# Attention key scores taken from 32 of the 128 partitions: one line of a two-layer transformer kernel

## The chip, the cores and the metric

The kernel runs on one core of one Trainium2 chip. The metric is device time in microseconds (us) of one execution. Engines are named PE (TensorE matmul), PEld (TensorE weight load, which the profile lists apart from the matmuls), DVE (VectorE), ACT (ScalarE), POOL (GpSimd) and SP (SyncE, whose queue issues most of the DMAs here).

## The reference, cut to what matters

The input is x of shape (4, 512, 128): four batches of 512 tokens. Layer 0 is causal attention with 16 heads of width 8, then a mixture of 8 experts; layer 1 is a linear recurrence with gates and two feed-forward blocks. Only the first attention is touched:

```
Q, K, V = (heads(WQ), heads(WK), heads(WV))          # (4, 16, 512, 8) each
score = jnp.einsum('bhqd,bhkd->bhqk', Q, K) / jnp.sqrt(jnp.asarray(D_K, x.dtype))
score = score + mask                                  # causal
score = score - jnp.max(score, axis=-1, keepdims=True)
score = jnp.exp(score)
score = score / jnp.sum(score, axis=-1, keepdims=True)
out = jnp.einsum('bhqk,bhkd->bhqd', score, V)
```

## The kernel before

**Steps.** The heads are worked in groups of four. Four batches of 512 tokens times four groups make 16 steps, numbered w (or G) from 0 to 15; g = w mod 4 is the group within its batch and b the batch. A batch is four tiles of 128 tokens.

**The padded operands.** A head has 8 numbers, but takes 32 partitions: 8 rounded values, again 8 rounded values, 8 of a low part, and 8 that carry padding (zeros or ones, and minus the row's maximum). So the four heads of a step fill 128 partitions. `QS` holds the queries of a step in this form, 128 partitions by 512 tokens. `QM` is `QS` plus minus the row maximum in the padding rows. `KP[:, w % 3, j, i, :]` holds the keys of token tile j and head i: the 32 partitions of head i are filled, the other 96 are zero. All three have the type float32r.

**Row scores** (`row_scores`, L1615) multiply `QS` of one query tile, as the stationary operand, with `KP` of one key tile and all four heads, 512 columns; ten such units make a step, four of them followed by a matmul that adds the causal mask (L1618). They go through three PSUM banks (0 to 2), and DVE takes the maximum over each (L1052).

**Key scores** (`key_scores`, L1631) do the same product turned round: the stationary operand is `KP` of one key tile and one head, and the moving operand is `QM`, from the tile's first query to the end. A step has 12 units n. Units 0 to 3 are key tile 0 of heads 0 to 3 (512 columns), units 4 to 7 are key tile 1 (384 columns), units 8 to 11 are key tiles 2 and 3 (one matmul of 256 columns and one of 128, into one bank). They use banks 3 to 5 in turn; unit n waits until ACT has taken the exponential of unit n - 3 (L679). The exponentials are the weights `PT`.

**Values** (`values`, L1643) multiply `PT` with the values `V` of a head: 128 rows and 32 output columns, four heads side by side in the four 32-partition parts of bank 6. These are plain float32, for which the trace lists two records each.

**Other PE work of a step:** four transposes of the maxima (`turn_max`, L1657), four of the outputs (`turn_out`, L1665), and in batches 1 to 3 the output projection, the transposes, the logits and the ranks of the batch before (L1671 to L1705).

**The order** of PE's work is written out by hand, L1738 to L1797, in this sequence for a step w:

```
turn_max(w), key_scores(w-1, 10), row_scores(w+1, 2), key_scores(w-1, 11), values(w-1, 1),
row_scores(w+1, 3), key_scores(w, 0), [times_wo | turn_normed | ranks], row_scores(w+1, 4),
key_scores(w, 1), row_scores(w+1, 5), key_scores(w, 2), row_scores(w+1, 6), key_scores(w, 3),
values(w-1, 2), values(w-1, 3), row_scores(w+1, 7), key_scores(w, 4), row_scores(w+1, 8),
key_scores(w, 5), turn_out(w-1), row_scores(w+1, 9), [project], values(w, 0), key_scores(w, 6),
key_scores(w, 7), [turn_heads | logits], key_scores(w, 8), row_scores(w+2, 0), key_scores(w, 9),
row_scores(w+2, 1)
```

In square brackets stands what only some steps have: `turn_heads` where w is 4, 8 or 12, `logits` where w is 6, 10 or 14. Step 15 has no row scores and step 14 has none of w+2.

Of the kernel before, what the change touches and what calls it, by code (L numbers as in the profile page):

```python
# [13 lines left out]
P = 128  # L14
NB = 4
TB = 4
SEQ = TB * P
# [19 lines left out]
ROWB = 3  # L37
KEYB = 3
# [70 lines left out]
def build(nc, d):  # L109
    ctx = ExitStack()  # L110
    with ctx:
# [95 lines left out]
        with ExitStack() as attention:  # L207
            def early(name, shape, dt=F32):
                return attention.enter_context(nc.sbuf_tensor(name, shape, dt))
# [8 lines left out]
            QM = early("QM", [P, 2, SEQ], F32R)  # L218
            KP = early("KP", [P, 3, TB, 4, P], F32R)
# [130 lines left out]
        bank = [ps[:, i, :] for i in range(8)]  # L350
# [1217 lines left out]
        def _(pe):  # L1568
# [53 lines left out]
            def key_scores(w, n):  # L1622

                c, i = n // 4, n % 4
                if n == 0:
                    pe.wait_ge(tp_free, TURNS["max", w] + 1)
                if NKU * w + n >= KEYB:
                    pe.wait_ge(exp_done, NKU * w + n - KEYB + 1)
                for j in KC[c]:
                    at = OFF[j] - OFF[KC[c][0]]  # L1630
                    mm = pe.matmul(bank[ROWB + n % KEYB][:, at:at + SEQ - j * P], KP[:, w % 3, j, i, :],  # L1631
                                   QM[:, w % 2, j * P:SEQ], start=True, stop=True)
                mm.then_inc(ts_full, 1)
            def values(w, j):

# [102 lines left out]
            for w in range(NW):  # L1738
# [3 lines left out]
                if w:  # L1742
                    key_scores(w - 1, 10)
                if rows_next:
                    row_scores(w + 1, 2)
                if w:
                    key_scores(w - 1, 11)
                    values(w - 1, 1)
                if rows_next:
                    row_scores(w + 1, 3)  # L1750
                key_scores(w, 0)
                if b and g == 1:
                    times_wo(b - 1)
# [308 lines left out]
            for t in (0, 1):  # L2062
                mm = pe.transpose(bank[6][:, t * P:(t + 1) * P], xp[:, t, :], ident)
            mm.then_inc(t_half, 1)
            pe.wait_ge(xp_done, 1)
            for t in (2, 3):
                mm = pe.transpose(bank[4][:, (t - 2) * P:(t - 1) * P], xp[:, t, :], ident)
# [110 lines left out]
```

## Time and profile before

| | us |
|---|---|
| median of 3 executions (lowest, highest) | 658.8 (657.65, 662.22) |
| the profiled execution, its own time | 656.35 |
| its span, from the first to the last instruction | 654.6 |
| TensorE clock granted, mean over the span | 0.965 of full speed |

| stretch of the span | what runs |
|---|---|
| 0 to 28 us | loads, first projections, first row scores |
| 28 to 212 us | the 16 steps of attention |
| 212 to 232 us | end of attention for the last batch |
| 232 to 323 us | the eight experts |
| 323 to 654.6 us | layer 1 |

The profile is of one execution. Matmuls are pipelined and their ends are modelled, so how long PE takes per matmul is read from the distance between the starts of two matmuls in a row, not from the duration of one. A weight load that starts at the same moment as the matmul before it was taken ahead, beside that matmul's work; one that starts with its own matmul was not.

### The profile page before, as it was taken

The numbers are of one execution on the slowest core, as the hardware profiler recorded it, in microseconds if no ns is written. First come the engines' busy times: TensorE is split into PE (matmuls) and PEld (weight loads), VectorE is DVE, ScalarE is ACT, GpSimd is POOL, SyncE is SP. The second block draws the span as 40 slices with busy tenths as digits, with TensorE's granted clock in tenths as the row PEclk, the third lists the DMA queues.
The fourth block names the chain that finished last, engine by engine and source line by source line (L and its number), as shares of the span: only waits on it lengthen the run. The fifth ranks groups of instructions, "written<-read, shape, count | busy, mean of one in ns | idle before, by whom it ended". The sixth has DMA issues, their size and how long they took to land.

```text
span 654.6 us, 9264 instructions
## 1 busy us (share of the span) xinstructions
PE 583.0 (89%) x3347; PEld 433.0 (66%) x3347; DVE 402.2 (61%) x958; ACT 316.2 (48%) x543; POOL 172.9 (26%) x185
## 2 busy tenths in 40 slices
PE   8889989999998379999649698899999999998997
PEld 3556556556564258787536476688778878786866
DVE  6778788798884511432248986884669556762430
ACT  4756566556665204534216243752575255643351
POOL 6112122452543630000058623611300041001100
PEclk9999999999999579999969798999999999999999
DMA  4773242243110455834111100100000000000000
GB/s 130 223 247 110 77 130 65 82 145 97 55 44 2 137 167 167 263 90 118 41 32 32 30 4 2 34 0 1 1 17 2 1 0 18 1 0 1 18 1 17
DMA packets 44926, 42.51 MB, mean 65 GB/s; under 512 B 4176, under 2 KB 34384, under 8 KB 44880
## 3 DMA queue, kind: packets, MB, share of 16 engines
q1 hardware_dynamic: 42544, 37.44, 18.8%
q0 software_dynamic: 2048, 4.20, 2.2%
q8 instruction: 27, 0.44, 0.3%
q10 hardware_dynamic: 288, 0.28, 0.2%
q14 instruction: 19, 0.16, 0.1%
HBM read 25.12 MB, written 16.78 MB: 64 GB/s over the span
## 4 chain that ended last, share of the span: by engine, by line
PE 66%; DVE 10%; ACT 7%; issue 6%; DMA 5%; POOL 4%; SPq 2%; DVEq 0%; POOLq 0%; ACTq 0%
PE ps L1945 7%; PE ps L1615 6%; PE ps L1898 5%; PE ps L1631 5%; PE ps L1643 5%; PE ps L1967 5%; PE ps L1968 4%; PE ps L1889 4%; PE ps L2048 4%; PE ps L2044 4%; PE ps L2045 4%; PE ps L1971 4%; PE ps L1961 2%; DMA XS<-xs_dram 2%; PE ps L1618 2%
## 5 line engine op out<-in xcount | busy, mean ns | idle before, releaser
L679 ACT ACTIVATE PT<-ps 128x384 f32<-128x384 f32 (+1 forms) x192 | 93.5, 529 | 69.9 <-PE ps L1631 67.5
L1052 DVE TENSOR_REDUCE pm<-ps 128x4 f32<-128x512 f32 x160 | 102.3, 681 | 10.0 <-PE ps L1615 9.4
L1615 PE MATMUL ps<-KP,QS 128*128 128x512 f32 x160 | 71.7, 452 | 7.9 <-DVEq L1045 2.5
L546 POOL TENSOR_SCALAR_AFFINE_SELECT PT<-PT 128x512 f32<-128x512 f32 x64 | 39.9, 636 | 129.1 <-ACT PT L679 129.1
L1631 PE MATMUL ps<-QM,KP 128*128 128x512 f32 (+3 forms) x256 | 69.1, 331 | 1.5 <-DVE QM L1066 1.1
L1631 PEld LDWEIGHTS ps<-QM,KP 128*128 128x128 f32 x256 | 43.8, 189 | 22.8 <-issue 12.6
L796 ACT ACTIVATE HT<-ps,cols 128x640 f32<-128x640 f32 x32 | 25.4, 795 | 54.8 <-PE ps L1889 54.8
L1615 PEld LDWEIGHTS ps<-KP,QS 128*128 128x128 f32 x160 | 29.8, 188 | 27.5 <-DVE pm L1052 11.5
L1414 DVE TENSOR_TENSOR_SCAN zero<-decay,OG 128x512 f32<-128x512 f32 x32 | 44.8, 1400 | 1.1
L1643 PE MATMUL ps<-PT,V 128*32 128x128 f32 (+3 forms) x512 | 44.6, 442 | 0.0
L521 POOL TENSOR_TENSOR rstd<-veps,mhalf 128x4 f32<-128x4 f32 x11 | 12.7, 1157 | 110.7 <-DVE veps L963 110.5
L1898 PE MATMUL ps<-W,HT 128*128 128x128 f32 x320 | 37.8, 277 | 2.9 <-ACT HT L796 2.9
L1898 PEld LDWEIGHTS ps<-W,HT 128*128 128x128 f32 x320 | 36.3, 192 | 4.8 <-ACT HT L796 4.8
L853 ACT ACTIVATE hF<-ps,cols 128x512 f32<-128x512 f32 x16 | 11.0, 689 | 56.1 <-PE ps L2048 56.1
L1889 PE MATMUL ps<-XST,W 128*128 128x320 f32 x128 | 36.5, 438 | 1.1 <-DVE XST L1315 1.1
L1409 DVE SCALAR_TENSOR_TENSOR OG<-ps,cols,vs 128x512 f32<-128x512 f32 x32 | 23.9, 748 | 18.6 <-ACT vs L832 14.1
L836 ACT ACTIVATE gs<-ps,half_bg 128x512 f32<-128x512 f32 x32 | 22.0, 688 | 25.7 <-PE ps L1971 25.5
L611 POOL DMA_INDIRECT G<-ys_dram,posG x8 | 7.6, 950 | 93.0 <-DMA ys_dram<-zero 90.8
L832 ACT ACTIVATE vs<-ps,cols 128x512 f32<-128x512 f32 x32 | 22.0, 688 | 20.0 <-PE ps L1971 19.8
L582 POOL DMA_INDIRECT G<-ys_dram,posG x24 | 29.6, 1234 | 6.8 <-issue 6.8
L1889 PEld LDWEIGHTS ps<-XST,W 128*128 128x128 f32 x128 | 22.4, 190 | 12.1 <-ACT HT L796 4.5
L1945 PEld LDWEIGHTS ps<-lwo,oT 128*128 128x128 f32 x256 | 29.1, 192 | 0.2
(300 smaller groups left out, 1309.2 us busy)
## 6 DMA issues: line engine op xcount, KB each, us to landing
qk_dram<-HL SPq DMA_DIRECT2D x24, 256.0 KB, 3.5
W<-in_eW SPq DMA_DIRECT2D x16, 256.0 KB, 3.6
QS<-qk_dram SPq DMA_DIRECT2D x15, 256.0 KB
KP<-qk_dram SPq DMA_DIRECT2D x60, 64.0 KB, 2.4
xs_dram<-zero SPq DMA_DIRECT2D x4, 640.0 KB, 3.5
XS<-xs_dram SPq DMA_DIRECT2D x8, 320.0 KB, 5.0
ys_dram<-zero SPq DMA_DIRECT2D x8, 320.0 KB, 2.9
whole_h_w<-in_h_w SPq DMA_DIRECT2D x2, 1024.0 KB, 9.7
```

What stands on the lines that cost most here:

```text
L546: g.affine_select(out=diag, in_=diag, pattern=[[0, 4], [1, P]], compare_op=ALU.is_ge, fill=0.0, base=0, channel_multiplier=-1).then_inc(se ...
L582: g.indirect_dma_start(out=G[:, b % 2, i, :], out_offset=None, in_=ys_dram, in_offset=bass.IndirectOffsetOnAxis(ap=posG[:, c:c + 1], axis= ...
L679: act.activation(PT[:, i, a:z], bank[ROWB + n % KEYB][:, 0:z - a], ACT.Exp, scale=float(DK) ** -0.5).then_inc(exp_done, 1)
L1052: v.tensor_reduce(pm[:, t, k, :], bank[n % ROWB].rearrange("p (i n) -> p i n", n=P), AXX, ALU.max).then_inc(row_free[n % ROWB], 1)
L1414: v.tensor_tensor_scan(st, decay[:, f:f + 1].to_broadcast([P, SEQ]), kv, 0.0, ALU.mult, ALU.add).then_inc(st_done, 1)
L1615: mm = pe.matmul(to, QS[:, G % 2, t * P:(t + 1) * P], KP[:, G % 3, k, :, :].rearrange("p i n -> p (i n)"), start=True, stop=t != k)
L1631: mm = pe.matmul(bank[ROWB + n % KEYB][:, at:at + SEQ - j * P], KP[:, w % 3, j, i, :], QM[:, w % 2, j * P:SEQ], start=True, stop=True)
L1643: mm = pe.matmul(bank[6][32 * i:32 * i + 32, j * P:SEQ], V[:, j * H + g * 4 + i, :], PT[:, i, OFF[j]:OFF[j + 1]], start=(j == 0), stop=(j ...
L1889: mm = pe.matmul(ps[:, 2 * (f % 2) + a, 0:HALF], W1[:, s, f * P:(f + 1) * P], XST[:, s, a * HALF:(a + 1) * HALF], start=True, stop=True)
L1898: mm = pe.matmul(bank[4 + j // 4][:, (j % 4) * P:(j % 4 + 1) * P], HT[:, s, f, j * P:(j + 1) * P], W2[:, s, f, :], start=(f == 0), stop=(f ...
L1945: mm = pe.matmul(bank[5][:, t * P:(t + 1) * P], src[:, f, t * P:(t + 1) * P], w[:, f, :], start=(f == 0 and t == 0), stop=(f == n - 1), sk ...
L1967: pe.matmul(to, high[n][:, cs], halves_of[:, 0, :], start=True, stop=False)
```

## The change

The two operands of the key scores' matmul are cut to the 32 partitions of head i. What is left out are products with the zeros of `KP`. `KP`, `QM`, their filling, the row scores and the order of the work stay as they are.

```
                 for j in KC[c]:
                     at = OFF[j] - OFF[KC[c][0]]
-                    mm = pe.matmul(bank[ROWB + n % KEYB][:, at:at + SEQ - j * P], KP[:, w % 3, j, i, :],
-                                   QM[:, w % 2, j * P:SEQ], start=True, stop=True)
+                    mm = pe.matmul(bank[ROWB + n % KEYB][:, at:at + SEQ - j * P], KP[32 * i:32 * i + 32, w % 3, j, i, :],
+                                   QM[32 * i:32 * i + 32, w % 2, j * P:SEQ], start=True, stop=True)
                 mm.then_inc(ts_full, 1)
```

## Rows read from the trace of the kernel before

**Rows 1.** The page: busy time by engine, and engines in 40 slices.
```profile
PE 583.0 (89%) x3347; PEld 433.0 (66%) x3347; DVE 402.2 (61%) x958; ACT 316.2 (48%) x543; POOL 172.9 (26%) x185
PE   8889989999998379999649698899999999998997
PEclk9999999999999579999969798999999999999999
```

**Rows 2.** Busy time in stretches; the first five each run between two groups of maxima transposes.
```profile
core 0: us, PE busy (x) PEld busy (x) DVE busy (x) ACT busy (x) POOL busy (x), PEclk, DMA share, GB/s
40.61:50.61 10.00, 10.00 (x72) 6.39 (x71) 8.68 (x17) 6.22 (x14) 2.27 (x4) 1.00 0.81 263
50.61:60.61 10.00, 10.00 (x72) 6.38 (x71) 8.20 (x17) 6.35 (x14) 2.49 (x5) 1.00 0.35 120
70.61:83.97 13.36, 12.38 (x80) 7.40 (x78) 8.87 (x18) 8.19 (x18) 2.72 (x5) 1.00 0.15 44
83.97:96.36 12.39, 11.50 (x80) 7.24 (x80) 10.69 (x29) 6.60 (x14) 3.27 (x5) 1.00 0.54 167
118.21:132.32 14.11, 12.94 (x79) 7.38 (x78) 10.26 (x25) 8.18 (x18) 7.54 (x10) 1.00 0.33 98
...
30.00:212.00 182.00, 173.37 (x1213) 108.25 (x1212) 144.72 (x376) 108.91 (x223) 58.83 (x84) 1.00 0.32 99
```

**Rows 3.** Instructions in order of time, step 1: same array shape.
```profile
start us, us, engine line op out<-in xcount [idle before <-releaser]
42.90 0.40 PE L1631 MATMUL ps<-QM,KP 128*128 128x512 f32 x1
42.90 0.19 PEld L1615 LDWEIGHTS ps<-KP,QS 128*128 128x128 f32 x1
43.14 0.39 PE L1615 MATMUL ps<-KP,QS 128*128 128x512 f32 x1
...
44.75 0.39 PE L1631 MATMUL ps<-QM,KP 128*128 128x512 f32 x1
```

**Rows 4.** The same view, into and out of the 32-column matmuls.
```profile
45.06 0.16 PEld L1643 LDWEIGHTS ps<-PT,V 128*32 128x32 f32 x8 [0.35 <-issue]
45.06 0.42 PE L1643 MATMUL ps<-PT,V 128*32 128x256 f32 x4
...
45.85 0.19 PEld L1615 LDWEIGHTS ps<-KP,QS 128*128 128x128 f32 x1 [0.20 <-issue]
45.85 0.50 PE L1615 MATMUL ps<-KP,QS 128*128 128x512 f32 x1
45.96 0.19 PEld L1631 LDWEIGHTS ps<-QM,KP 128*128 128x128 f32 x1
46.19 0.34 PE L1631 MATMUL ps<-QM,KP 128*128 128x384 f32 x1
```

**Rows 5.** The same view: a full group of values, then key scores.
```profile
47.79 1.06 PE L1643 MATMUL ps<-PT,V 128*32 128x512 f32 x8
...
48.24 0.61 PE L1643 MATMUL ps<-PT,V 128*32 128x512 f32 x4
48.78 0.79 PE L1631 MATMUL ps<-QM,KP 128*128 128x384 f32 x4
```

**Rows 6.** The same view: after a matmul of 128 columns, and full-array transposes.
```profile
50.03 0.19 PEld L1615 LDWEIGHTS ps<-KP,QS 128*128 128x128 f32 x1
50.09 0.44 PE L1615 MATMUL ps<-KP,QS 128*128 128x512 f32 x1
50.38 0.39 PE L1618 MATMUL ps<-mask,identr 128*128 128x512 f32 x1
...
50.61 0.27 PE L1657 MATMUL ps<-const,MX 128*128 128x128 f32 x1
```

**Rows 7.** Waits from 30 to 212 us: us in total, times, longest.
```profile
PEld ps L1615 <- DVE pm L1052: 10.6, 18, 1.3
PEld ps L1631 <- ACT PT L679: 3.8, 12, 0.8
PE ps L1615 <- DMA KP<-qk_dram: 1.9, 1, 1.9
```

**Rows 8.** The line of the key scores, its matmuls: count, and when.
```profile
L1631 PE MATMUL ps<-QM,KP x256: 220/339/507, 29.8 to 209.6; 128*128 128x256 f32 x64, 128*128 128x512 f32 x32, 128*128 128x384 f32 x32
```

## The prediction

> **What bounds the kernel now.** I read the page first: PE is busy for 89% of the span and nearly all through attention [rows 1]. The line that changes runs only from 29.8 to 209.6 us, as 256 matmuls, 16 per step [rows 8], so only attention's 182 us can move. Then the stretches between two groups of maxima transposes, that is, one step each: steps 1 and 2 take 10.00 us both, with PE busy throughout, DVE for 8.2 to 8.7 us and ACT for 6.3; steps 4, 5 and 8, which also carry projections and the batch before, take 12.4 to 14.1 us and leave PE idle 0.9 to 1.2 us each [rows 2]. The clock granted is 1.00 there, the 2.4 GHz level. Over 30 to 212 us PE is idle 182.0 - 173.4 = 8.6 us. So PE bounds attention, and in the plain steps a nanosecond more on PE is one more in the span. The chain of waits agrees: its largest parts are PE's lines.
>
> Since ends are modelled, I read what a matmul occupies from starts. Two 512-column matmuls of the full array stand 0.24 us apart, 0.23 in most places (42.90 to 43.14; 50.38 to 50.61), and the second one's weight load starts with the first matmul: it is hidden [rows 3, 6].
>
> **Part 1: the work itself.** The number of matmuls, their columns and their weight columns (128) stay. In the trace a matmul's start-to-start time follows its moving columns, and nothing in it depends on rows, which are 128 in every form listed. I take 0 for having fewer rows.
>
> **Part 2: changing the shape of the array.** Today key scores and row scores both use 128 rows by 128 columns. After the change the key scores use 32 by 128, and they stand between full-array work nearly everywhere. No matmul of fewer than 128 rows is in the trace, so the price is bounded from both sides. The nearest rows are the values, 128 by 32.
> - Going in: a key score at 44.75 is followed by values at 45.06, 0.31 us later (up to 0.33 elsewhere) instead of 0.23, and their weight load starts only then [rows 3, 4]. The array is drained first: about 0.10 us.
> - Coming out: the values' second pass of 512 columns starts at 48.24, 0.45 us after the first at 47.79, of which 0.02 is the first one's exposed load, so a pass takes 0.43. The next key score starts 0.54 us after the second, at 48.78 [rows 5]: 0.10 again.
> - The load after a change is bare. At 45.85 load and matmul start together, the following load only at 45.96, and the following matmul at 46.19, 0.34 us later instead of 0.23 [rows 4]. That is 0.11 us for 128 weight columns, less for values' 32.
> It is the shape and not the data type that costs: the float32 transposes at 50.61 follow a float32r matmul by 0.23 us [rows 6].
> So a change into a shape with 128 weight columns costs 0.10 + 0.11, rounded to 0.20 us, if 32 rows behave as 32 columns do. The low end is 0, if the row slice is only a mask. Above, I know no dearer row.
>
> The Trainium skill, page "TensorEngine Tiling (Array Packing)", section Key Properties, says that changing the tiling mode, as opposed to the tile, drains TensorE. By that rule the 0.10 holds for rows as well; the trace shows it for columns only.
>
> **Part 3: how many changes are added.** I count in the written order. A plain step has ten runs of key scores: 10; 11; 0; 1; 2; 3; 4; 5; 6 to 8; 9. Each has an entry and an exit, 20 changes. Three of them are there already: values after 11, values after 3, values before 6. So 17 are new: 9 entries and 8 exits. Steps 4, 6, 8, 10 and 12 have full-array work between 7 and 8: 19 each. Step 0 has no units 10 and 11 of a step before: 15. Step 14 has logits between 7 and 8, but no row scores between 8 and 9: 17. Step 15 has no row scores: 4. In sum 15 + 8 x 17 + 5 x 19 + 17 + 4 = 267.
>
> Of these, 43 are exits after a 128-column matmul. There the next load is already half bare: row scores at 50.09 are followed by the mask at 50.38, 0.29 instead of 0.23 [rows 6]. They cost 0.20 - 0.06 = 0.14 us. The other 224 cost 0.20.
> 224 x 0.20 + 43 x 0.14 = 44.8 + 6.0 = **50.8 us** more on PE.
>
> **Part 4: what covers it.** PE's waits in this stretch are on DVE's maxima (10.6 us by its weight loads), on ACT's exponentials (3.8) and once on the keys' DMA (1.9) [rows 7]; these lists overlap with hidden time, and idle is 8.6. A slower PE reaches those points later while DVE and ACT need the same time, so most of it goes: I take 6.5 us, bounds 0 and 8.6. DVE has 1.3 us of slack in a plain step and gains 3.4, ACT more, so neither becomes the bound. What stays is where PE's own product starts the chain it waits for (q and k projections to ACT, DVE, then the bank).
>
> **Part 5: neighbours.** Only units 6, 7 and 8 stand side by side, on other rows and other banks. If they overlap, a unit's 384 columns (0.16 us) and a bare load (0.06) can go, at most twice a step, if ACT frees the banks in time: 16 x 0.44 = 7 us at best, 0 at worst. I take 2, because unit 8 waits for the exponential of unit 5.
>
> DMAs, their queues and POOL: no issue is added or moved. The loads of KP and QS wait on key scores and transposes that come later, but in a plain step they have 10 us and are needed a step ahead; 0. Layer 1 and the experts are the same work, later: 0.
>
> **Sum.** 50.8 - 6.5 - 2 = +42.3 us, against the profiled execution's own 656.35: 698.7. The median of 658.8 is 2.4 us above that execution; put on the median it is 701, and I forecast **700 us**.
>
> **The rivals.**
> (a) *The row slice is only a mask: no drain, loads stay hidden.* For it: row and column slices are different things in the array, and the trace has no row slice. Against it: the one partial shape in the trace pays at both borders. Then only part 5 is left: 0 to -7 us, some 657 us. Chance 0.12 for no change within 1%.
> (b) *The other side: side-by-side units overlap fully.* Place: units 6 to 8 of each step. Price: 0.44 us a step, 7 us in all, plus whatever time banks come free earlier; 651 us. It decides only if (a)'s condition holds and unit 8 finds its bank free. For it: values on four different column parts start 0.01 us apart, as the eight records within 1.06 us show, where two passes of 0.43 would fill the time alone [rows 5]. Against it: only 3 of 12 units have such a neighbour. Chance 0.04.
> The skill's page "TensorE: Matmul & The Clock Gate", Part 3, says that matmuls on different row groups run at once, and that four of 32 rows and 512 columns were 3.07 times as fast; here the full-array work between the units leaves that rule little to act on.
> (c) *Half the price: a drain, but loads still taken ahead* (or the reverse). 267 x 0.10 = 27 us, less 5 of waits and 2: +20, 679 us. For it: drain and load are two effects, and only their sum at values is sure. Chance 0.08.
> (d) *Dearer: the float32r product takes twice as long on 32 rows,* or the clock falls in the thinner stretches. 16 x 5120 columns more at 0.23 us per 512 are +37 us, 735 to 740 us. Nothing in the trace speaks for it. Chance 0.04.
> (e) The forecast: 0.72. That the slice is not a slice, because the operands are widened again, is in (a).
>
> **How the numbers follow.** Within the forecast: waits absorbed 0 to 8.6, neighbours 0 to 7, and 0.18 to 0.21 per change give about +30 to +53, 688 to 711. About 1% is what a measurement of this kernel can tell from no change. The range takes in the forecast with its bounds and (c): 671 to 714, and leaves out (a), (b) and (d), 0.20 in all. Slower by over 1%: (c), (d), (e), 0.84. Within 1%: 0.12. Faster: 0.04.
>
> **What would show it.** In the changed kernel's trace the key score's weight load starts with its own matmul instead of with the one before it, and so does the row score's load after it. A row score stands 0.33 us after a 512-column matmul in front, and its successor 0.34 after it. Plain steps take about 13.3 us instead of 10.0. If the loads stay hidden and the starts 0.23 apart, parts 2 and 3 are wrong and (a) or (b) holds. If only one of the two effects is there, it is (c). If key scores of 512 columns stand over 0.4 us from their successor with its load hidden, it is (d). The DVE waits for row scores should grow, and PE's waits for DVE shrink; if they don't, part 4 is wrong.

## The result, and the profile after

The changed kernel takes 723.3 us in the median of four executions (718.57, 728.07, 717.66 and 731.92), the kernel before 658.2; the ratio is 1.095, 95% interval 1.083 to 1.108. Forecast were 700 us and a range of 671 to 714. The direction was right, the size was not. The profiled execution took 718.57 us.

The comparisons leave out executions whose granted clock is clearly lower than that of their fellows; since the clock is part of the question here, I list all executions where it matters.

The page of the changed kernel: busy time, and the clock granted in 40 slices of the span.

```profile
PE 648.4 (90%) x3347; PEld 442.4 (62%) x3347; DVE 405.8 (57%) x958; ACT 319.8 (45%) x543; POOL 172.8 (24%) x185
...
PEclk9967999756999996699998798999999999999999
```

Against [rows 1] the new thing is in the clock: two dips, to 0.6 in the 3rd and 4th slice and to 0.5 in the 8th to 10th. Those slices are in attention, where the kernel before had none. The later dip at slices 16 and 17, where attention ends, was there before, at slices 14 and 15. In the trace's own times the clock stood at half from 34.5 to 37.9, from 44.7 to 61.8 and from 133.4 to 174.4 us in attention; the first of these is too short to stand out in a slice.

Now the order of time in a plain step at full clock (columns: start us, duration us, engine, line, what, then idle before it):

```profile
65.41 0.19 PEld L1615 LDWEIGHTS ps<-KP,QS 128*128 128x128 f32 x1 [0.62 <-issue]
65.41 0.50 PE L1615 MATMUL ps<-KP,QS 128*128 128x512 f32 x1
65.84 0.18 PEld L1631 LDWEIGHTS ps<-QM,KP 32*128 32x128 f32 x1 [0.24 <-issue]
65.84 0.49 PE L1631 MATMUL ps<-QM,KP 32*128 32x512 f32 x1
66.26 0.19 PEld L1615 LDWEIGHTS ps<-KP,QS 128*128 128x128 f32 x1 [0.24 <-issue]
66.26 0.50 PE L1615 MATMUL ps<-KP,QS 128*128 128x512 f32 x1
66.37 0.19 PEld L1618 LDWEIGHTS ps<-mask,identr 128*128 128x128 f32 x1
...
66.60 0.40 PE L1618 MATMUL ps<-mask,identr 128*128 128x512 f32 x1
66.92 0.18 PEld L1631 LDWEIGHTS ps<-QM,KP 32*128 32x128 f32 x1 [0.37 <-issue]
```

This answers to [rows 3, 4]. Every change between 128 and 32 rows now does what only the values did before: the load starts with its own matmul instead of with the one before. Mask to key score takes 0.32 us (66.60 to 66.92) instead of 0.23: a drain of 0.09 to 0.10. Key score to row score takes 0.42 (65.84 to 66.26): 0.23, a bare load of 0.10 and a drain of 0.09. So a change costs 0.19 to 0.20 us, as forecast.

The run of units 6 to 8, in the same view:

```profile
72.73 1.07 PE L1643 MATMUL ps<-PT,V 128*32 128x512 f32 x8
73.73 0.30 PEld L1631 LDWEIGHTS ps<-QM,KP 32*128 32x128 f32 x4 [0.84 <-issue]
73.73 0.45 PE L1631 MATMUL ps<-QM,KP 32*128 32x384 f32 x4
74.11 0.19 PEld L1615 LDWEIGHTS ps<-KP,QS 128*128 128x128 f32 x1
```

Four matmuls with 1152 columns (384, 384, 256 and 128) end within 0.45 us; in [rows 5] they took 0.79. From the values' start to the next row score's own work it is 1.38 (72.73 to 74.11) plus a bare load of 0.11 here, and 1.62 (57.79 to 59.41, shown with units 6 to 8 below) plus 0.05 before: 0.18 less, although an exit of 0.14 is paid in it. The three heads run at once, and the stretch is 0.32 us shorter than it would be without that.

Not all of this reaches the step. Unit 9, the next key score, waits for the first exponential:

```profile
74.75 0.29 PEld L1631 LDWEIGHTS ps<-QM,KP 32*128 32x128 f32 x2 [0.45 <-ACT PT L679]
```

It starts 2.02 us after the values (72.73 to 74.75), exactly as in the kernel before (57.79 to 59.81). There the row score in front of it stood 0.40 us ahead, where 0.23 is enough, so 0.17 us of waiting was hidden behind a modelled end although PE is shown busy. So in a plain step the two changes on this stretch, 0.14 and 0.20 us by the forecast's prices, cost nothing: an estimate from these starts is that 0.17 went into the old wait and 0.17 was paid by the overlap.

The stretches, each one step: step 1 (at 43.03), step 2, step 7 and step 8, with columns as in [rows 2].

```profile
43.03:62.91 19.88, 19.88 (x71) 8.75 (x70) 9.16 (x18) 6.44 (x13) 2.42 (x4) 0.57 0.43 137
62.91:75.69 12.78, 12.63 (x71) 6.19 (x70) 8.32 (x16) 6.58 (x14) 2.49 (x5) 1.00 0.27 94
132.94:154.74 21.80, 21.80 (x86) 10.12 (x85) 11.22 (x33) 6.72 (x14) 2.49 (x4) 0.51 0.09 24
154.74:179.08 24.34, 23.86 (x80) 11.00 (x78) 9.06 (x17) 8.25 (x17) 7.32 (x9) 0.60 0.19 56
```

The third column from the end is the clock: a plain step at clock 1.00 takes 12.78 us, one at 0.57 takes 19.88. And at half clock the same instructions stand like this:

```profile
49.49 0.80 PE L1615 MATMUL ps<-KP,QS 128*128 128x512 f32 x1
...
50.08 0.63 PE L1618 MATMUL ps<-mask,identr 128*128 128x512 f32 x1
50.64 0.28 PEld L1631 LDWEIGHTS ps<-QM,KP 32*128 32x128 f32 x1 [0.65 <-ACT PT L679]
...
51.36 0.29 PEld L1615 LDWEIGHTS ps<-KP,QS 128*128 128x128 f32 x1 [0.44 <-issue]
```

Key score to row score is 0.72 us (50.64 to 51.36) instead of 0.42. The clock granted is 0.50 here: this is the lower level, 1.2 GHz.

The three slow steps would take 12.8, 13.1 and 16.0 us at full clock (the lengths of steps 2 and 11 here, and of step 8 in a later execution of the same kernel). So the clock cost 7.1 + 8.7 + 8.3 = 24 us in them. The dip at 34.5 us lies in step 0, which took 14.80 us; with 64 rows (below), where that step had no dip, it took 13.24. That is 1.6 more, about 26 us of 718.57 in all, and without them this execution would have taken about 693. That splits the 62 us between the two profiled executions (718.57 - 656.35) into 36 for the changes of shape, 2 of which lie behind step 14, and 26 for the clock. The split is an estimate from the lengths of steps.

### The profile page after: what moved, and what is told of

Its sections match the earlier page's. It is cut to its first block, busy times and chain, and to the rows that moved or that the text cites. A ratio compares the mean times of both kernels' runs of the same rounds, so it can differ in the third digit from the quotient of the medians.

```text
span 716.8 us, 9264 instructions
## 1 busy us (share of the span) xinstructions
PE 648.4 (90%) x3347; PEld 442.4 (62%) x3347; DVE 405.8 (57%) x958; ACT 319.8 (45%) x543; POOL 172.8 (24%) x185
## 4 chain that ended last, share of the span: by engine, by line
PE 75%; ACT 7%; DVE 7%; issue 5%; POOL 3%; DMA 1%; DVEq 0%; POOLq 0%; ACTq 0%
PE ps L1631 9%; PE ps L1615 9%; PE ps L1643 6%; PE ps L1945 6%; PE ps L1898 5%; PE ps L1889 5%; PE ps L1967 4%; PE ps L2048 4%; PE ps L2044 4%; PE ps L1968 4%; PE ps L2045 4%; PE ps L1971 3%; PE ps L1618 2%; PE ps L1961 2%; PE ps L1665 1%
## 5 line engine op out<-in xcount | busy, mean ns | idle before, releaser
L679 ACT ACTIVATE PT<-ps 128x384 f32<-128x384 f32 (+1 forms) x192 | 96.9, 529 | 126.1 <-PE ps L1631 125.7
L1052 DVE TENSOR_REDUCE pm<-ps 128x4 f32<-128x512 f32 x160 | 105.4, 685 | 42.6 <-PE ps L1615 28.1
L1615 PE MATMUL ps<-KP,QS 128*128 128x512 f32 x160 | 86.2, 543 | 4.3 <-DVEq L1045 2.7
L1631 PE MATMUL ps<-QM,KP 32*128 32x512 f32 (+3 forms) x256 | 82.0, 418 | 2.6 <-DVE QM L1066 1.0
L1631 PEld LDWEIGHTS ps<-QM,KP 32*128 32x128 f32 x256 | 40.1, 200 | 61.0 <-issue 44.7
L1615 PEld LDWEIGHTS ps<-KP,QS 128*128 128x128 f32 x160 | 32.5, 205 | 37.9 <-issue 27.8
L1643 PE MATMUL ps<-PT,V 128*32 128x128 f32 (+3 forms) x512 | 51.8, 504 | 0.0
L796 ACT ACTIVATE HT<-ps,cols 128x640 f32<-128x640 f32 x32 | 25.4, 795 | 56.4 <-PE ps L1889 56.4
L1898 PE MATMUL ps<-W,HT 128*128 128x128 f32 x320 | 37.9, 278 | 3.2 <-ACT HT L796 3.2
L1889 PE MATMUL ps<-XST,W 128*128 128x320 f32 x128 | 38.2, 453 | 1.1 <-DVE XST L1315 1.1
```

The source lines that it names most:

```text
L679: act.activation(PT[:, i, a:z], bank[ROWB + n % KEYB][:, 0:z - a], ACT.Exp, scale=float(DK) ** -0.5).then_inc(exp_done, 1)
L1052: v.tensor_reduce(pm[:, t, k, :], bank[n % ROWB].rearrange("p (i n) -> p i n", n=P), AXX, ALU.max).then_inc(row_free[n % ROWB], 1)
L1615: mm = pe.matmul(to, QS[:, G % 2, t * P:(t + 1) * P], KP[:, G % 3, k, :, :].rearrange("p i n -> p (i n)"), start=True, stop=t != k)
L1643: mm = pe.matmul(bank[6][32 * i:32 * i + 32, j * P:SEQ], V[:, j * H + g * 4 + i, :], PT[:, i, OFF[j]:OFF[j + 1]], start=(j == 0), stop=(j ...
L1889: mm = pe.matmul(ps[:, 2 * (f % 2) + a, 0:HALF], W1[:, s, f * P:(f + 1) * P], XST[:, s, a * HALF:(a + 1) * HALF], start=True, stop=True)
L1898: mm = pe.matmul(bank[4 + j // 4][:, (j % 4) * P:(j % 4 + 1) * P], HT[:, s, f, j * P:(j + 1) * P], W2[:, s, f, :], start=(f == 0), stop=(f ...
```

## The experiments

All ran beside the kernel before, whose medians were 656.9 to 657.8 us and whose granted clock was 0.960 to 0.969. Two chips were used, numbered 7 and 11: the first pair of grouped kernels, the doubled row scores and the last kernel ran on 7, all others on 11; for the first executions of the changed kernel the chip is not on record. Two theories of the clock were put against each other. A: it falls because the array stands empty in drains and bare loads. B: it falls because products on few rows keep too little of the array at work.

### The changed kernel again

> The changed kernel once more, on the chip and beside the runs it is compared with: 715 to 735, mean clock 0.89 to 0.93, as in its first four executions. If the clock on this chip stays at 0.96, the falls were that chip's, and it takes about 693.

Measured: 693.93, 704.05, 720.16 and 728.12 us, at mean clocks of 0.962, 0.943, 0.913 and 0.907. The clock differs from execution to execution of one program, and time follows it. Only the execution of 704.05 us has a trace: there the clock was at half from 35.0 to 38.4 and from 127.2 to 144.2 us. The one of 693.93 has a mean clock like the kernel before, so attention must have run at full clock nearly throughout, and it takes 36 us more than before (657.7). I take that as the price of the change itself, without the clock; the forecast's sum had been 42.

### 64 rows instead of 32

```diff
-KP[32 * i:32 * i + 32, w % 3, j, i, :], QM[32 * i:32 * i + 32, w % 2, j * P:SEQ]
+KP[64 * (i // 2):64 * (i // 2) + 64, w % 3, j, i, :], QM[64 * (i // 2):64 * (i // 2) + 64, w % 2, j * P:SEQ]
```

> The key scores take 64 rows (their own head's and its neighbour's, whose keys are zero there) instead of 32. Same 267 added changes of the array's shape. In the changed kernel plain steps took 12.8 us at full clock, and 54 us of attention ran at half clock. Theory A (the clock falls because the array stands empty in the drains and bare weight loads): as the changed kernel, mean clock 0.89 to 0.93, time 715 to 730. Theory B (the clock falls because a product on 32 rows keeps only a quarter of the array at work): with 64 rows it falls less or not, clock above 0.945, time 695 to 712. Both: plain steps at full clock 12.7 to 13.1 us. If 64 rows were no change of shape: 658.

Measured: 708.16, 689.89, 709.76 and 707.42 us, clocks 0.941, 0.970, 0.936 and 0.942. Plain steps at full clock 12.76 us. In order of time:

```profile
65.96 0.49 PE L1631 MATMUL ps<-QM,KP 64*128 64x512 f32 x1
...
66.38 0.19 PEld L1615 LDWEIGHTS ps<-KP,QS 128*128 128x128 f32 x1 [0.24 <-issue]
```

0.42 us again, with the load bare: half the rows is a change of shape at the same price. Units 6 to 8 overlap less here, since 6 and 7 (heads 2 and 3) have the same 64 rows:

```profile
72.75 0.62 PE L1631 MATMUL ps<-QM,KP 64*128 64x384 f32 x4
...
73.77 0.29 PEld L1631 LDWEIGHTS ps<-QM,KP 64*128 64x128 f32 x2 [0.29 <-ACT PT L679]
```

Yet unit 9 starts 2.02 us after the values (71.75) once more, and the plain step is as long as with 32 rows. The rest of the overlap with 32 rows is only time spent waiting for ACT. The clock lies higher than with 32 rows, where seven of eight executions had 0.896 to 0.943 and one 0.962, but falls still happen (42.3 to 59.3 and 189.0 to 209.5 us in the trace). This leans to B and does not decide.

### Changes of shape without narrow work

```diff
+if n in (0, 1, 2, 4, 5, 8, 9, 10):
+    pe.matmul(bank[ROWB + n % KEYB][:, 0:16], KP[32 * i:32 * i + 32, w % 3, KC[c][0], i, :],
+              QM[32 * i:32 * i + 32, w % 2, 0:16], start=True, stop=True)
 for j in KC[c]:
     ...
```

> The kernel before, all key scores on 128 rows; eight units of a step (0, 1, 2, 4, 5, 8, 9, 10) are preceded by an extra product of 32 rows and 16 columns into the same bank, which the real one then overwrites. That makes 16 changes of shape per step, 17 in the changed kernel, but leaves the real work on full rows. Both theories: 256 changes at 0.17 to 0.20 us less some waits, +38 to +46 us at full clock, plain steps 12.7 to 13.3 us. Theory A (empty time lowers the clock): mean clock 0.89 to 0.93, time 715 to 735. Theory B (quarter-filled products lower it): clock as before, 0.96 to 0.97, time 696 to 706.

Measured: 693.3 us (692.70 to 695.56), ratio 1.056, interval 1.052 to 1.061, clocks 0.962 to 0.967. The clock by slices, then a plain step:

```profile
PEclk9999999999999985999996989999999999999999
```

```profile
54.20:67.19 12.99, 12.99 (x80) 7.67 (x78) 8.42 (x16) 6.60 (x14) 2.50 (x4) 1.00 0.30 92
```

16 changes of shape a step, against 17 in the changed kernel, and steps of 12.99 us against 10.00, so 2.99 / 16 = 0.19 us a change. The trace has no dip in attention, and the mean clock of all four executions is that of the kernel before. A falls: empty time of this size does not lower the clock, on the chip on which the changed kernel had 0.907 to 0.962. It also prices the changes alone: +36 us.

### The same columns added on 128 rows, and on 32

Every row score done twice (on 128 rows), in the changed kernel:

```diff
 t, k = UNITS[u]
+pe.matmul(to, QS[:, G % 2, t * P:(t + 1) * P],
+          KP[:, G % 3, k, :, :].rearrange("p i n -> p (i n)"), start=True, stop=True)
 mm = pe.matmul(to, QS[:, G % 2, t * P:(t + 1) * P],
     ...
```

> The changed kernel with every row score's matmul done twice into the same bank (the second overwrites the first): 160 more products on the full array, about 0.22 us each, +35 us of PE time, with the same 267 changes. Theory B (the clock falls because too little of the array is at work): the falls in attention go or shrink, mean clock 0.955 to 0.97, time 693 + 30 to 35 = 723 to 730, hardly more than the changed kernel's own 718 to 732 that lacks this work. Theory A (empty time as such): drains are as many, the share of time in them falls from about 0.28 to 0.23, so falls may shrink a little, clock 0.90 to 0.95, time 740 to 765.

And every 32-row product of the key scores done twice:

```diff
-mm = pe.matmul(bank[ROWB + n % KEYB]...)
+for _ in range(2):
+    mm = pe.matmul(bank[ROWB + n % KEYB]...)
```

> The changed kernel with every 32-row product of the key scores done twice in a row into the same bank: 5120 more columns a step, as many as doubling the row scores added, but on 32 rows instead of 128. Same 267 changes. Theory B (clock falls because too little of the array is at work): more and longer falls than in the changed kernel, mean clock 0.85 to 0.90, time above 745. Theory A (empty time as such): the share of empty time falls just as in the run with doubled row scores, so clock 0.955 as there, 725 to 735.

Measured: on 128 rows 729.92, 727.11, 725.31 and 735.15 us at clocks of 0.958, 0.959, 0.962 and 0.946; on 32 rows 768.97, 785.87, 766.93 and 766.87 us at 0.899, 0.876, 0.901 and 0.901. A plain step at full clock, first of the kernel with the work on 128 rows, then of the one with 32, the latter with its next two steps, in which the clock was down:

```profile
58.56:73.43 14.87, 14.87 (x82) 7.62 (x81) 8.41 (x16) 6.59 (x13) 2.49 (x4) 1.00 0.22 79
```

```profile
46.23:61.18 14.95, 14.87 (x88) 7.82 (x87) 9.08 (x18) 6.67 (x13) 2.50 (x4) 1.00 0.57 183
61.18:81.06 19.88, 19.88 (x87) 10.30 (x86) 8.41 (x16) 6.72 (x14) 2.50 (x4) 0.70 0.17 59
81.06:105.62 24.56, 24.47 (x88) 11.96 (x86) 8.51 (x16) 6.66 (x13) 2.50 (x4) 0.55 0.14 49
```

The clock by slices, first the kernel with the work on 128 rows, then the one on 32:

```profile
PEclk9999999999999995699999699999999999999999
```

```profile
PEclk9998577999985589858999978999999999999999
```

The two kernels have the same 267 changes, the same 5120 added columns a step and the same step length at full clock, within 0.08 us. They differ in the rows of the added work, and by 39 us in the median. The 128-row work made the kernel it was added to slower by 9 us (median 728.5, against 719.4 over that one's eight executions), though it is worth 16 x 2.1 = 34 us at equal clock. Both speak for B. They also differ in the chip, 7 for the 128-row work and 11 for the other, and the changed kernel was not run on 7, so this pair alone leaves the chip as a rival. What does not hang on it are the runs on chip 11: 0.962 to 0.967 with changes of shape alone, 0.907 to 0.962 with the key scores on 32 rows, 0.876 to 0.901 with them done twice.

### The price per change, on part of the units

32 rows for units 0 to 3 alone, or for units 6 to 8 alone:

```diff
+r = slice(32 * i, 32 * i + 32) if n <= 3 else slice(0, P)         # the other run: 6 <= n <= 8
+mm = pe.matmul(..., KP[r, w % 3, j, i, :], QM[r, w % 2, j * P:SEQ], start=True, stop=True)
```

> 32 rows for units 0 to 3 alone: four entries and three exits a step are new, about 107 of the 267 changes. Price per change of 0.17 to 0.20 us: +16 to +21 us, plain steps 11.2 to 11.4 us, 674 to 680 with the clock as before. Theory A: clock falls little or not with 40 percent of the empty time, 674 to 685. Theory B: the same, but with more falls, since these are the longest key scores (512 columns): 680 to 695.

Measured: 679.0 us, ratio 1.035 (1.030 to 1.039), clocks 0.954 to 0.959. Plain steps 11.36 to 11.40 us: 1.38 / 7 = 0.197 us a change. The time is at the top of what the price alone gives; the clock dipped at 32.2 to 39.0 us, where the kernel before ran at 1.00, and step 0 took 15.6 us against 12.2.

> 32 rows for units 6, 7 and 8 alone. Entry from the values is there already, so one exit a step is new, and two changes in six steps with work between 7 and 8: 27 in all, 4 to 5 us. In the changed kernel these units started 0.00 us apart where their banks were free, which saves up to two units of 384 columns, 0.3 to 0.5 us a step. Theory (price per change, gain per neighbour): 652 to 658, no change within 1 percent or slightly faster. Rival (any slice lowers the clock in attention): 665 or more.

Measured: 658.0 us, ratio 1.001 (0.999 to 1.003), plain steps 10.00. No change, and the view in order of time says why:

```profile
58.16 0.45 PE L1632 MATMUL ps<-QM,KP 32*128 32x384 f32 x4
58.54 0.19 PEld L1615 LDWEIGHTS ps<-KP,QS 128*128 128x128 f32 x1
...
58.64 1.64 ACT L679 ACTIVATE PT<-ps 128x384 f32<-128x384 f32 x4 [1.75 <-PE ps L1632]
59.18 0.30 PEld L1632 LDWEIGHTS ps<-QM,KP 128*128 128x128 f32 x2 [0.45 <-ACT PT L679]
```

The same stretch of the kernel before (its values start at 57.79, those of the other at 57.17):

```profile
57.79 1.07 PE L1643 MATMUL ps<-PT,V 128*32 128x512 f32 x8
...
59.26 1.64 ACT L679 ACTIVATE PT<-ps 128x384 f32<-128x384 f32 x4 [1.75 <-PE ps L1631]
59.41 0.44 PE L1615 MATMUL ps<-KP,QS 128*128 128x512 f32 x1
59.81 0.30 PEld L1631 LDWEIGHTS ps<-QM,KP 128*128 128x128 f32 x2 [0.27 <-ACT PT L679]
```

PE is through with the three units earlier (1.37 us after the values' start instead of 1.62), but ACT starts its exponentials 1.47 us after it in both, and unit 9 waits for the first of them. It starts 2.01 and 2.02 us after the values, with 0.45 and 0.27 us of idle in front. The overlap was turned into a wait, as in the changed kernel.

### Fewer changes: a grouped order

Key scores in four runs of three (9 to 11, 0 to 2, 3 to 5, 6 to 8), three of the runs next to values, so five changes are added in a plain step. The order of one step:

```
turn_max(w), row_scores(w+1, 2), key_scores(w-1, 9..11), values(w-1, 1), row_scores(w+1, 3..4),
key_scores(w, 0..2), values(w-1, 2..3), row_scores(w+1, 5..6), key_scores(w, 3..5),
row_scores(w+1, 7), turn_out(w-1), row_scores(w+1, 8..9), values(w, 0), key_scores(w, 6..8),
row_scores(w+2, 0..1)
```

> Key scores on 32 rows, and PE's order rewritten so that they come in four runs of three units (9 to 11, 0 to 2, 3 to 5, 6 to 8), three of them next to values: 5 added changes in a plain step instead of 17. By the runs so far a change costs 0.17 to 0.20 us, and neighbours on other rows run at once: three units of 512, 512 and 512 columns in the time of one. So 10.0 + 5 x 0.18 - 1.4 - 0.5 for short bare loads = 9.0 us a plain step, or DVE's 8.7 if that binds, against 10.0 before: 16 x -0.9 = -14 us, 643. Theory A (empty time lowers the clock): clock as before. Theory B (partly filled rows lower it): three quarters of the rows are at work when three units overlap, so little or no fall, 640 to 655; with falls 660 to 680. Rival: the new order brings waits for the exponentials and eats the gain: 655 to 665 at full clock.

> The same order as the run with grouped 32-row key scores, but on 128 rows: tells the order's own cost from the rows'. Nothing overlaps and nothing is drained: 10.0 us a plain step if no wait appears. Expected 655 to 665; if the order makes waits for exponentials, 665 to 680, and the 32-row run is to be read against this one.

Measured: on 32 rows 672.2 us, ratio 1.023 (1.020 to 1.026), clock 0.945 to 0.953, plain steps 10.3; on 128 rows 667.6 us, 1.016 (1.012 to 1.019), plain steps 10.66. Both are slower, by 1 to 3 percent, and the rival was right that waits appear, though not for the exponentials themselves: ACT copies the sums behind an exponential, and the transposes wait for the copy. So the next pair moved that copy ahead of the exponential of unit 3 and `turn_out` behind row score 8:

> The grouped order with 32 rows, but the transposes of the outputs one row score later, and ACT's copy of the sums ahead of the exponential of unit 3: in the first grouped run PE stood idle 0.8 to 1.1 us a step for that copy (11.6 us by weight loads of the transposes). Without that wait plain steps take 9.4 to 9.7 us, 652 to 660 with the clock at 0.953. If another wait takes its place, 665 as before.

> The same improved order on 128 rows. Control: 655 to 662 if the order costs nothing more; the 32-row run beats it by 0.4 to 0.8 us a plain step at full clock, if overlap pays more than the five added changes.

Measured: 32 rows 660.8 us, ratio 1.006 (1.004 to 1.009), clock 0.950 to 0.955; 128 rows 659.0 us, 1.003 (1.001 to 1.004), clock 0.962 to 0.966. In order of time on 32 rows:

```profile
73.03 0.19 PEld L1631 LDWEIGHTS ps<-QM,KP 32*128 32x128 f32 x3 [0.37 <-issue]
73.04 0.50 PE L1631 MATMUL ps<-QM,KP 32*128 32x512 f32 x3
73.47 0.16 PEld L1643 LDWEIGHTS ps<-PT,V 128*32 128x32 f32 x8 [0.25 <-POOL PT L546]
```

Three products of 512 columns end 0.50 us after they start, the duration of one. A plain step, on 32 rows and on 128:

```profile
60.63:70.18 9.55, 9.45 (x70) 4.75 (x71) 7.89 (x17) 5.92 (x14) 2.48 (x5) 1.00 0.35 124
```

```profile
60.66:70.59 9.93, 9.93 (x71) 6.30 (x71) 7.95 (x17) 5.92 (x14) 2.47 (x5) 1.00 0.35 119
```

The overlap gains 0.4 us in a plain step, and the whole loses it again. Steps 0 to 14 together take 173.5 us in both grouped kernels and 171.6 in the kernel before: step 8 takes 15.3 and 15.2 us against 14.1, which is the order's cost, and with 32 rows steps 0 and 1 are 1.3 us longer than with 128, the clock being at half from 39.8 to 43.2 us. Behind step 14 the 32-row kernel is 2 us longer, with the clock down from 203.6 instead of 219.4 us.

One more reading bears on the clock. The first grouped kernel on 128 rows has a dip in attention too, from 39.7 to 43.1 us, though none of its key scores is on fewer rows:

```profile
39.00:44.00 5.00, 4.82 (x23) 3.48 (x24) 3.34 (x6) 1.56 (x4) 0.99 (x2) 0.66 0.85 258
```

It follows the wait for the keys' DMA. So a short fall at that place doesn't need narrow products; the falls of 17 us and more in attention were seen with narrow products alone.

### The grouped order only where it paid

> The improved grouped order with 32 rows in steps 2, 3, 5, 9 and 13 alone, where a step was 0.4 to 0.8 us shorter than in the kernel before (9.57, 9.55, 11.59, 11.42 and 11.46 against 10.0, 10.0, 12.39, 12.08 and 12.1 us); the other steps keep the order and the 128 rows of the kernel before. If steps keep these lengths: -3.0 us, 654 to 656, ratio 0.995. If the borders between the two orders cost a change or a wait each (up to 8 borders at 0.2 to 0.3 us): no gain, 656 to 659. The clock should stay at 0.96 or above by theory B, since 32-row products run three at a time.

Measured: 655.4 us against 657.0, ratio 0.998, interval 0.996 to 0.9997, clock 0.960 to 0.965. Step 2 took 9.37 us, step 3 9.55, step 5 11.58, step 9 11.26, step 13 11.27. The gain over the kernel before, 0.2 percent, is only just clear of zero. The other steps kept their lengths within 0.3 us but for step 1, which still has the old order: it grew from 10.0 to 11.5 in the profiled execution, where the clock was at half from 40.3 to 43.7 us, ahead of its first product on 32 rows. That ate nearly half of what the five steps gained (3.5 us).

## Why the prediction was right and wrong

**What bounds the kernel, part 1.** Right. Of 62 us between the profiled executions 60 lie in steps 0 to 14, and fewer rows made no product shorter: doubling the key scores added 14.95 - 12.78 = 2.17 us a step on 32 rows, doubling the row scores 2.09 on 128, each for ten times 512 columns.

**Part 2, the price of a change.** Right: 0.19 to 0.20 us, drain 0.09 to 0.10 and bare load 0.10, in the changed kernel, with 64 rows (0.42 between starts), with the extra products (0.19) and on units 0 to 3 (0.197). It was taken from 32 columns and held for 32 and 64 rows. The rule from the Trainium skill's page "TensorEngine Tiling (Array Packing)", section Key Properties, that changing the mode drains TensorE, is so shown for rows as well.

**Part 3, the count.** Right. Between consecutive matmul records the changed kernel's attention has 360 changes of shape, the kernel before 95: 265 more, and 267 were counted. 17 changes give 3.2 us a plain step; measured are 2.77. Of the difference 0.34 is the stretch ahead of unit 9, and 0.1 says that a change cost 0.19 rather than 0.20.

**Part 5, neighbours.** Right in size, but not by its reasoning. I took 2 us, because unit 8 might not find its bank free; in plain steps it did, and the stretch got 0.32 us shorter. What held the gain down was unit 9's wait for the first exponential, which the prediction did not have: only about 0.17 us a step, 3 us in all, was left. The Trainium skill's page "TensorE: Matmul & The Clock Gate", Part 3, has matmuls on different row groups run at once; the trace agrees, with three heads of 512 columns in 0.50 us. On its own the overlap was worth nothing, as the run with units 6 to 8 shows.

**Part 4, what covers it.** A little under-sized. At full clock the changed kernel costs 36 us. The 50.8 us are 49 at the price per change that the plain step shows (3.11 us for its 17), and 3 go for the neighbours, so about 10 us of waits went, where I took 6.5 with a bound of 8.6. The sign that I had named came: DVE's waits for row scores grew from 6.0 to 25.4 us, and the weight loads' waits for DVE shrank from the 10.6 of [rows 7] to 1.1 (slow stretches included). The steps show where: step 5, which has idle time in [rows 2], grew by 1.8 us in place of 2.8, step 8 by 1.9 in place of 3.2, steps 9 and 13 by 1.6 and 1.5. The bound was too low because it counted only the time in which PE is shown idle: the 0.17 us ahead of unit 9 is a wait that a modelled end hides, some 3 us over 16 steps.

**The step that failed** is one that the sum did not have as a term. The prediction says "The clock granted is 1.00 there, the 2.4 GHz level", and carries it over to the changed kernel. The clock stood only in rival (d), "or the clock falls in the thinner stretches", with the words "Nothing in the trace speaks for it" and a chance of 0.04 together with another case, from whose doubled columns its price was taken. By the mean clocks it fell in seven of eight executions (0.896 to 0.943, against 0.960 to 0.969 for the kernel before), and it cost about 26 us in the profiled one. The range ended at 714 because the bounds of the forecast were all bounds on work, none on the speed at which it runs. With the clock's fall the sum is 656.35 + 36 + 26 = 718; without it, about 693, it would have lain within the range and 7 us under the forecast.

What stays open: why the clock fell in one execution and not in another of the same program, and why at 34.5, 44.7 and 133.4 us. The fall at 44.7 comes after PE stood idle for the keys' DMA at the end of step 0 (the stretch from 40 to 44 us has it busy for 2.65). The kernel before has that wait too [rows 7] and kept its clock; the first grouped kernel on 128 rows lost it there for 3.4 us, where this one lost it for 17. That a pause starts such a fall and narrow products keep it going would fit, but no run tests it. Ahead of the falls at 34.5 and 133.4 us there was no such pause.

## What to carry to other kernels

Cutting a contraction to the rows it needs makes no single product faster, and each border with full-array work cost 0.2 us; it can pay only where several such products on different rows stand side by side and fill the array together, and where the engine that empties their banks is ready for them. Count the borders in the issue order before anything else. And when a change takes rows or columns out of a dense stretch, put a term for the clock into the sum and into the range: the same cut lowered it on top of its own price.

## What the runs showed of the hardware

A weight load of another number of rows was not taken ahead of the running matmul, whether for 32 or 64 rows: after a change of shape it started with its own matmul, and the change cost 0.19 to 0.20 us. Loads of the same shape were taken ahead where the matmul in front was running, with 0.23 us from start to start. Matmuls on different 32-row parts and in different banks started less than 0.01 us apart, and three of 512 columns took the time of one, 0.50 us.

Long falls of the clock in attention came with products on few rows and not with short stops: 256 changes of shape left the mean clock at 0.962 to 0.967, while 5120 more columns a step, added to the changed kernel, gave 0.876 to 0.901 on 32 rows and, on another chip, 0.946 to 0.962 on 128. How few rows, and for how long, no run shows. One program gave mean clocks from 0.896 to 0.962, so one execution of such a kernel says little about its time.
